# Projection and experts of a transformer tail put into one stage, with the projection's matmuls spread through the experts' chain

## The reference

```python
def _L1_ffn_ref(x, W, b, A, Bmat, LiMEs):        # x is the layer-normalised x
    H = jnp.einsum('btd,od->bto', x, W) + b       # d = o = 512
    z = jnp.einsum('btd,dr->btr', x, A)           # r = 32
    anchors = jnp.arange(1, T, 2)
    H_slice = H[:, anchors, :8]
    delta_slice = jnp.einsum('bar,er->bae', z[:, anchors], LiMEs)
    H_scale = jnp.maximum(jnp.max(jnp.abs(H_slice)), EPS)
    d_scale = jnp.maximum(jnp.max(jnp.abs(delta_slice)), EPS)
    logits = 0.5 * (H_slice / H_scale) + 0.5 * (delta_slice / d_scale)
    probs = softmax(logits)
    thresh = top_k(probs, 2)[0][..., -1:]
    weights = probs * sigmoid((probs - thresh) / 0.5)
    weights = weights / (sum(weights) + 1e-9)
    p_mix = jnp.einsum('bte,er->btr', repeat(weights, 2), LiMEs)
    return H + jnp.einsum('btr,ro->bto', z * p_mix, Bmat) * 0.5
```

## Time and profile before

| what | us |
|---|---|
| median of three runs (798.72 to 800.43) | 799.75 |
| the profiled execution | 799.84 |
| its span, from the first to the last instruction | 797.8 |
| TensorE busy in the span | 691.3 |
| VectorE | 622.4 |
| ScalarE | 482.2 |
| GpSimd | 364.8 |

### The profile page before, as it was taken

One profiled execution on the slowest core, in us unless ns is written; L12 is line 12 of the kernel. 1 busy time (PEld: TensorE's weight loads), 2 busy tenths in 40 slices (PEclk: granted clock), 3 DMA queues, 4 the chain that ended last, 5 costly groups with the idle time before them and its releaser, 6 DMA issues. The chain is left out here.

```text
span 797.8 us, 17690 instructions
## 1 busy us (share of the span) xinstructions
PE 691.3 (87%) x6633; PEld 358.0 (45%) x6633; DVE 622.4 (78%) x1031; ACT 482.2 (60%) x870; POOL 364.8 (46%) x271
## 2 busy tenths in 40 slices
PE   4999999999967875699999489999999999389944
PEld 2454455545545654244444144444444444145541
DVE  6888788888636676699998398999999999355456
ACT  3878876676436665476776167878788787422100
POOL 2000039999725563022112257767686767333100
PEclk9999999999999998799999779999999999779955
DMA  6235455656253320134332100000000000045305
GB/s 161 77 132 171 154 177 151 152 135 173 55 146 72 83 68 6 21 75 75 75 67 57 31 0 2 1 2 1 2 1 1 2 1 1 1 80 80 53 1 210
DMA packets 94183, 54.90 MB, mean 69 GB/s; under 512 B 78548, under 2 KB 78548, under 8 KB 94100
## 3 DMA queue, kind: packets, MB, share of 16 engines
q1 hardware_dynamic: 93348, 53.25, 26.7%
q10 hardware_dynamic: 752, 0.52, 0.3%
HBM read 32.20 MB, written 4.19 MB: 46 GB/s over the span
## 5 line engine op out<-in xcount | busy, mean ns | idle before, releaser
L1312 POOL TENSOR_TENSOR query_qn<-query_eq,query_rq 128x1024 f32<-128x1024 f32 x64 | 121.8, 1904 | 56.7 <-DVE query_rq L1246 54.9
L558 ACT ACTIVATE keys_ek<-keys_psK,keys_mk 128x512 f32<-128x512 f32 x128 | 86.9, 684 | 38.9 <-DVE keys_mk L411 37.0
L411 DVE TENSOR_REDUCE keys_mk<-keys_psK 128x2 f32<-128x1024 f32 x64 | 77.9, 1217 | 16.7 <-PE keys_psK L617 16.6
L1237 DVE TENSOR_REDUCE query_mq<-query_psQ 128x16 bf16<-128x1024 f32 x64 | 75.6, 1181 | 5.2 <-PE query_psQ L1380 5.0
L1243 DVE TENSOR_REDUCE query_lq<-query_eq 128x16 f32<-128x1024 f32 x64 | 77.2, 1207 | 2.6 <-ACT query_eq L1321 2.5
L1321 ACT ACTIVATE query_eq<-query_psQ 128x1024 f32<-128x1024 f32 x64 | 65.2, 1019 | 22.5 <-PE query_psQ L1393 22.5
L628 PE MATMUL keys_psT<-all_ident,keys_ek 128*128 128x128 f32 x512 | 70.8, 282 | 0.0
L1402 PE MATMUL query_psX<-all_ident,query_qn 128*128 128x128 f32 x512 | 70.7, 282 | 0.0
L1040 POOL TENSOR_SCALAR ff_hr<-ff_h,ff_qs 128x1376 f32<-128x1376 f32 x16 | 22.7, 1416 | 104.4 <-DVE ff_qs L1087 104.4
L640 PE MATMUL keys_psG<-keys_eT,keys_cT 128*64 128x512 f32 x256 | 69.0, 617 | 1.0 <-issue 0.9
L628 PEld LDWEIGHTS keys_psT<-all_ident,keys_ek 128*128 128x128 f32 x512 | 55.5, 142 | 28.2 <-issue 20.0
(11 more groups left out here) (246 smaller groups left out, 1438.6 us busy)
## 6 DMA issues: line engine op xcount, KB each, us to landing
all_ring<-in_L_ffn_w_down_dram SPq DMA_DIRECT2D x8, 688.0 KB, 4.7
all_ring<-in_L_ffn_w_gate_dram SPq DMA_DIRECT2D x10, 512.0 KB, 4.9
all_ring<-in_L_ffn_w_up_dram SPq DMA_DIRECT2D x10, 512.0 KB, 3.9
all_x_res<-in_x_dram SPq DMA_DIRECT2D x4, 1024.0 KB, 6.1
att_ctx_n<-in_ctx_dram SPq DMA_DIRECT2D x16, 256.0 KB, 2.9
out_dram<-all_x_res SPq DMA_DIRECT2D x16, 256.0 KB, 2.2
all_cf<-in_ctx_dram SPq DMA_DIRECT2D x15, 256.0 KB, 2.6
att_w_nat<-in_L_ffn_W_dram SPq DMA_DIRECT2D x4, 256.0 KB, 4.5
```

Of the source, the lines that this page charges most:

```text
L411: dve.tensor_reduce(mk[:, c, :], psK[c % 2][:, :, :], X, ALU.max, negate=True).then_inc(mk_ok, 1)
L558: act.activation(ek[t % 2][b][:, c, :], psK[c % 2][:, b, :], ACT.Exp, bias=mk[:, c, b:b + 1], accum_out=le[t % 2][:, b, c:c + 1]).then_inc ...
L1237: dve.tensor_reduce(mq[g % 2][:, :, 0:HEADS], psQ[g % 2][:, :, :].rearrange("p b (h d) -> p b h d", d=D), X, ALU.max, negate=True).then_in ...
L1312: pool.tensor_tensor(qn[m % 2][:, :, :], eq[m % 3][:, :, :], rq[m % 2][:, :].unsqueeze(2).broadcast_to([P, 2 * HEADS, D]), ALU.mult).then_ ...
```

## The change

One stage `projection_and_experts` takes the place of the two, and `x_T` is kept for all 16 tiles. Per tile TensorE does z (12 passes of 128 columns), then only the eight router columns of H in eight narrow passes, into `psR`. ScalarE copies both out (`zT`, `raw`). Of H itself ten tiles (`product_of`) are computed through two banks `psH`, four passes per tile of the loop and the rest between the steps of the chain; ScalarE copies them to `hb` and GpSimd adds them to the residual. H of the other six tiles goes straight into the bank in which `bm_parts` is added. `dl` is done for four tiles at a time in the loop. High parts are made four tiles ahead. GpSimd adds five products after its 16 bias additions and the other five only after `done_v` 5, the end of the chain. VectorE does `zp` of two groups at once, and the low part of the next group before the last results of a group. The core of the diff, with the new code of each engine:

```diff
-def projection(nc, a, k):
-def experts(nc, a, k):
+def projection_and_experts(nc, a, k):
+    FILL = 4
+    AHEAD = 3
+    product_of = [0, 1, 4, 8, 5, 9, 2, 6, 3, 7]
+    FIRST = 5
+    order = [4 * g + q for q in range(4) for g in range(4)]
+    added = [TILES + product_of.index(t) + 1 if t in product_of else t + 1 for t in range(TILES)]
+        x_T = s.sb("x_T", [P, TILES, 2 * NC, P], F16)
+        psD = [psA, psH[0], psH[1], psB]
+        w_head = k.WT[:, :, :, 0:EXPERTS]
...
+        def _(pool):
+            for t in range(TILES):
+                pool.wait_ge(xs_ok, t + 1)
+                pool.tensor_tensor(k.x[:, t, :], k.x[:, t, :], k.b_full[:, :], ALU.add).then_inc(b_ok, 1)
+            pool.wait_ge(b_ok, TILES)
+            for n in range(FIRST):
+                add_product(n)
+            pool.wait_ge(done_v, 5)
+            for n in range(FIRST, PRODUCTS):
+                add_product(n)
...
+        def _(act):
+            for i in range(AHEAD + 1):
+                high(i)
+            for i in range(TILES):
+                if i + AHEAD + 1 < TILES:
+                    high(i + AHEAD + 1)
+                act.wait_ge(z_ps, i + 1)
+                act.activation(zT[:, i, :], psR[:, 2 + i % 2, 0:P], ACT.Copy, scale=1.0 / W_SCALE).then_inc(z_ok, 1)
+                act.wait_ge(n_ps, i + 1)
+                act.activation(raw[:, i, :, :], psR[:, i % 2, 0:2 * EXPERTS].rearrange("p (m e) -> p m e", m=2),
+                               ACT.Copy).then_inc(raw_ok, 1)
+                if i % 3 == 2:
+                    product(i // 3)
+            product(5)
+            act.wait_ge(done_v, 3)
+            act.activation(e[:, :, :], lg[:, :, :], ACT.Exp).then_inc(act_ok, 1)
+            product(6)
+            act.wait_ge(done_v, 4)
+            act.activation(w[:, :, :], u[:, :, :], ACT.Exp, scale=-2.0).then_inc(act_ok, 1)
...
+        def _(dve):
+            for i in range(TILES):
+                low(i)
+                if i + 2 < TILES:
+                    normed(i + 2)
...
+            scaled(0)
+            scaled(1)
+            rest(0)
+            for q in range(4):
+                for g in range(3 if q < 2 else 2):
+                    result(4 * q + g)
                 if q < 3:
+                    rest(q + 1)
+                if q < 2:
+                    scaled(q + 2)
+                for g in range(3 if q < 2 else 2, 4):
+                    result(4 * q + g)
...
+                for c in range(NC):
+                    pe.matmul(head, hi[c], w_head[:, :, c, :], start=c == 0, stop=False, skip_group_check=True)
+                for c in range(NC):
+                    mm = pe.matmul(head[:, 0:EXPERTS], lo[c], w_head[:, 0, c, :], start=False, stop=c == NC - 1,
+                                   skip_group_check=True)
+                mm.then_inc(n_ps, 1)
+                if i < TILES - 1:
+                    products(FILL * i, FILL * i + FILL)
+                if i > 0 and i % 4 == 0:
+                    z_limes(i - 4, i)
...
             for n, t in enumerate(order):
+                bank = psD[n % 4]
+                if n in (1, 2):
+                    pe.wait_ge(hb_ok, PRODUCTS - 2 + n)
+                wait(pe, o_ok, n - 3)
+                if t not in product_of:
+                    for m in range(4 if n == 3 else 0, 3 * NC):
+                        projected(t, bank, m, False)
                 pe.wait_ge(z_fin, n // 4 + 1)
+                pe.matmul(bank[:, :], zs[:, t % 4, t // 4, :], k.bm_parts[:, :], start=t in product_of,
+                          stop=True).then_inc(d_ps, 1)
```

More of the change, by code:

```diff
@@ new lines, in _ @@
+                    normed(i + 2)
+            dve.memset(ones2[:, :], 1.0).then_inc(lnk, 1)
+            dve.memset(wf[:, :, :], 0.0).then_inc(lnk, 1)
+            n[0] += 2
+            dve.wait_ge(lnk, n[0])
+            dve.wait_ge(raw_ok, TILES)
+            link(dve.scalar_tensor_tensor(out=Hs[:, :, :], in0=raw[:, :, 0, :], scalar=1.0 / W_SCALE,
+                                          in1=k.b_full[:, 0:EXPERTS].unsqueeze(1).broadcast_to(TE), op0=ALU.mult, op1=ALU.add))
+            link(dve.scalar_tensor_tensor(out=Hs[:, :, :], in0=raw[:, :, 1, :], scalar=1.0 / W_SCALE, in1=Hs[:, :, :],
+                                          op0=ALU.mult, op1=ALU.add))
@@ new lines, in rest, with result @@
+            def rest(q):
+                dve.wait_ge(zs_ok, q + 1)
+                dve.tensor_tensor(zs[D:P, q, :, :], zp[D:P, q, :, :], zs[D:P, q, :, :], ALU.subtract).then_inc(z_fin, 1)
+            def result(m):
+                t = order[m]
+                dve.wait_ge(b_ok, added[t])
+                dve.wait_ge(d_ps, m + 1)
+                dve.scalar_tensor_tensor(out=k.x[:, t, :], in0=psD[m % 4][:, :], scalar=1.0 / W_SCALE,
+                                         in1=k.x[:, t, :], op0=ALU.mult, op1=ALU.add).then_inc(o_ok, 1)
@@ L1644, in _ @@
+            scaled(0)
+            scaled(1)
+            rest(0)
             for q in range(4):
+                for g in range(3 if q < 2 else 2):
+                    result(4 * q + g)
                 if q < 3:
-                    product(q + 1)
-                dve.wait_ge(zs_ok, q + 1)
-                dve.tensor_tensor(tiles(zs, q)[D:P], tiles(zp, q)[D:P], tiles(zs, q)[D:P], ALU.subtract).then_inc(z_fin, 1)
-                for n in range(4 * q, 4 * q + 4):
-                    dve.wait_ge(d_ps, n + 1)
-                    t = order[n]
-                    dve.scalar_tensor_tensor(out=k.x[:, t, :], in0=psD[n % 4][:, :], scalar=1.0 / W_SCALE,
-                                             in1=k.x[:, t, :], op0=ALU.mult, op1=ALU.add).then_inc(o_ok, 1)
@@ L1666, in _, with parts_of @@
-        @block.sync
-        def _(sp):
-            for n, t in enumerate(order):
-                sp.wait_ge(o_ok, n + 1)
-                sp.dma_start(out[t], k.x[:, t, :]).then_inc(store, 16)
-            sp.wait_ge(store, 16 * TILES)
+                    rest(q + 1)
[3 more added lines that the diff above has]
+                    result(4 * q + g)
         @block.tensor
         def _(pe):
-            for t in range(TILES):
-                mm = pe.matmul(psA[:, t * EXPERTS:(t + 1) * EXPERTS], k.zT[0:RANK, t, :], k.limesT[:, :],
-                               start=True, stop=True)
-            mm.then_inc(a_ps, 1)
+            def parts_of(t):
+                hi = [x_T[:, t, c, :] for c in range(NC)]
+                lo = [x_T[:, t, NC + c, :] for c in range(NC)]
+                return hi, lo
@@ new lines, in projected, with products @@
+            def projected(t, bank, m, stop):
+                hi, lo = parts_of(t)
+                xT, wt = ((hi, k.WT_hi), (hi, k.WT_lo), (lo, k.WT_hi))[m // NC]
+                return pe.matmul(bank[:, :], xT[m % NC], wt[:, m % NC, :], start=m == 0, stop=stop)
+            def products(first, last):
+                for j in range(first, last):
+                    n, m = j // (3 * NC), j % (3 * NC)
+                    if m == 0:
+                        wait(pe, hb_ok, n - 1)
+                    mm = projected(product_of[n], psH[n % 2], m, m == 3 * NC - 1)
+                    if m == 3 * NC - 1:
+                        mm.then_inc(h_ps, 1)
```

216 lines of the change are left out of this document (98 added, 118 removed).

## The result

The changed kernel takes 775.6 us in the median of four runs (774.49 to 777.45); beside it the kernel before took 799.24 (798.62 to 800.43). The ratio is 0.9702 with a 95% interval of 0.9685 to 0.9719: 3% faster. The forecast was 782.1 with a range of 777 to 789. The profiled execution took 775.0 us.

What follows compares the result with a forecast made beforehand. TensorE's queue was taken to carry nearly all the tail: from 701.13, 70.8 us of passes, 2.7 of low clock and 1.8 of waits reach 776.4; last result, store and surroundings make 782.1, likely cases 777 to 789.

Steps and rivals of the forecast that it cites:

- the fill covers the chain: VectorE chain, L1600 to L1626: 35 wide TensorE passes, 7.6 us, stand beside its 7.5 us, leaving some 0.3 us for hand-over.
- The rival of 814 us: From the chain's first link on: clock falls to 0.50, 148 wide passes cost 0.216 more each, 32.0 us; chance 0.04.
- router's heads: Eight narrow passes per tile in the loop: 128 at 0.056 us, 7.2 us, with bounds of 0.030 and 0.101 each.
- weights' spread: Spreading the experts' weights (L1691 before): 32 passes at 0.112 us, 3.6 us, with bounds of 0.050 and 0.160 each.
- dl, 32 passes: dl matmuls (L1676 before), 24 of them now in the projection: 0.112 us each, 3.6 us.
- low clock at the start: TensorE from the first z at 701.13 to 706.40: the lower clock costs half of 5.3 us, 2.7.
- waits: TensorE's remaining waits: 0.3 at the chain, 0.3 at wT copies, 0.2 around z_fin, 1.0 at the results; 1.8 us in all.
- the case at 787.9: Router's head passes each cost their weight load, 0.101 us, adding 5.8 us; chance 0.12.
- cheap small passes: Head passes at 0.030 us (3.3 less, 2.9 let through) and spread at 0.050 (2.0 less): 777.2; chance 0.15.
- these five additions: GpSimd's last five product additions, behind done_v 5, when VectorE mostly reads psum: costed at nothing.
- The feeding loop: VectorE and GpSimd preparing tiles: 2.21 us per tile against TensorE's 2.20, hence nothing on the sum.
- the slack at tile 15: Last tile of the loop: its transpose lands at 734.2, TensorE comes at 736.2, two microseconds of slack.

Runs made afterwards that it cites:

- e4: Changed kernel with the 44 wide passes between the chain's steps issued ahead of its first link: 789.22 us, ratio 0.9868 to the kernel before.
- e3: Changed kernel with each tile's eight narrow head passes done twice: 779.31 us, ratio 0.9745 to the kernel before.
- e2: Kernel before the change, with the spread's matmuls rotating over the row strips and the first product waiting for all four groups: 799.9 us (one run).
- e1: Changed kernel with the spread's matmuls in the old order, four in a row on the same row strip: 782.7 us (one run).
- e5: Changed kernel with GpSimd's last five additions no longer waiting for the chain's end: 778.28 us, ratio 0.9732 to the kernel before.
- e11: Changed kernel plus 18 unread warm-up passes, bias additions waiting for the third tile after their own, one product added before the chain: 777.9 us.
- e6: Changed kernel plus 18 unread wide TensorE passes while it would wait for the first transpose: 775.89 us, ratio 0.9702 to the kernel before.
- e10: The changed kernel again, unaltered, beside the runs with extra passes on the same chip: 777.70 us, ratio 0.9729 to the kernel before.
- e8: Changed kernel without the bias in the residual, GpSimd setting one element per tile instead of adding: 775.6 us (one run).

## Why the prediction was right or wrong

**Right: what bounds the kernel and where the gain comes from.** TensorE's idle time went, the clock stayed at 1.00, and the fill covers the chain: 35 passes stand in 737.20 to 744.71, 7.5 us, as worked out. e4 shows the worth of the passes between the links, 9.3 us of cover and some 3 of clock. The four wide passes of a tile, the z passes, the last result and the first hand-overs have their forecast sizes. The rival of 814 us counted 60 products after the first link; 50 stand there in the order, which makes 812, and e4 shows that it would not have come.

**The sum against the trace.** From TensorE's first z pass to its last the prediction has 701.13 to 776.56, 75.43 us; the trace has 699.67 to 769.95, 70.28. The difference of 5.15 by its terms:

| term | forecast | measured | difference |
|---|---|---|---|
| router's heads, 128 passes | 7.2 | 3.3 | -3.9 |
| weights' spread, 32 passes | 3.6 | 1.1 | -2.5 |
| dl, 32 passes | 3.6 | 4.0 | +0.4 |
| low clock at the start | 2.7 | 2.4 | -0.3 |
| waits (measured: what is left) | 1.8 | 2.9 | +1.1 |

The first two tiles took 5.88 us where two at the full clock take 3.47; that is the 2.4. Behind the last result the store took 2.43 us instead of 2.7, and the stage began 1.5 us sooner: together 773.2 instead of 780.0 for the span.

**The failed steps are the two prices of small passes.** The sum took 0.056 for a head pass, "the nearest row, which contains a full load of this kind; fewer columns cannot make it dearer unless the load itself does". It is 0.025 (e3), below even the lower bound of 0.030. The wrong step was to read 0.056 as what the weight load needs. The load is hidden behind its neighbours: one lasts 0.10 us in this trace too, and four head passes with their four loads begin 0.10 after each other (728.56, 728.66, 728.76 for the two groups and the fill). The columns fit as what costs 0.056 for a pass with 128 of them (0.056 x 2.4 GHz = 134 cycles); that was not tried by itself. Sixteen and eight columns cost 0.025 alike, the distance of the 64x64 passes in the earlier trace rows, a row that I had in hand and took as a bound, rounded up. The rule of the Trainium skill, "TensorE: Matmul & The Clock Gate", LDWEIGHTS, by which 128 columns of weights load in P/1.2 = 107 ns, describes one load's duration well (0.10 here) and not the rate of consecutive passes; the case at 787.9 was wrong by a factor of four in the price.

The spread was put at 0.112 with a lower bound of 0.050. It is 0.034 (1.10/32). I had seen that neighbouring passes use other row strips and gave it no number; e2 and e1 give it, a factor of 2.4 at either clock, strips and banks together. The rival "cheap small passes" (777.2, chance 0.15) is what came, and both of its prices were still too high.

**Waits: 1.8 against 2.9.** By the distances of starts the chain's links cost the 0.3 forecast, the copies of wT 0.27 (0.3 forecast) and a bank wait in the results 0.58 (1.0 forecast). The first `bm_parts` pass comes 0.67 late instead of 0.2, and two items are in no forecast: 0.66 before the second group's `bm_parts` pass, which waits for its `rest` too (752.78 to 753.65), and some 0.36 before the four groups of dl. The first `bm_parts` pass waits for `rest`, and `rest` took 1.26 instead of 0.69. That is the addition behind `done_v` 5 beside it: in e5, where none runs, that part is 0.57 shorter. The prediction put these five additions "behind done_v 5, when VectorE mostly reads psum", and cost them "at nothing"; `rest` reads sbuf. The same with the fifth addition before the chain: the first Hs step took 0.95 instead of 0.29, within the 0.55 to 1.3 us allowed. It cost nothing: in e11, where that step took 0.29, VectorE waited 0.71 us for dl instead.

**The feeding loop: right, and nearer than it looked.** A tile costs VectorE and GpSimd 2.01 us instead of the 2.21 that I had worked out: normed is stopped (1.37), low isn't (0.68), the addition takes 1.65 and the next begins 0.36 later. The Trainium skill, "SBUF — State Buffer", SBUF: two separate sides, has this stop for a VectorE instruction with one tensor input when it runs in a two-port mode; normed is stopped in the loop, and two `tensor_scalar` steps in e5, while no run shows the mode itself. TensorE's tile is 1.74 and a quarter of 1.0 for dl, 1.99 us. So both queues run at the same pace, and TensorE's 2.4 us of low clock gave the loop its slack. That is why the slack at tile 15 was the 2 us forecast (its low part ended at 726.26 and its z began at 731.36, with 3.1 for the transpose), and why e6, which takes the low clock away, wins 0.8.

**The range.** It was built from costs alone. The stage's start differs by up to 2.6 us between profiles of this one kernel (693.76, 694.43, 696.38), and a median by 2.1. The lower bound should have held that too. Which side of that bound a median falls on is partly chance: with the start of the kernel before, 1.5 us later, the profiled execution would have taken 776.5, still half a microsecond below the range, and e10's median of 777.7 lies inside it, with the same two prices wrong.

## What to carry to other kernels

Price a narrow matmul from the distance between starts of the narrowest passes in the trace, not from a weight load's duration or a wider pass, and let few-row f32 matmuls of one group rotate over the row strips and psum banks (the two were never tried apart). Before removing a loss on the bounding engine, compare the pace of the engine that feeds it: here the two were 1% apart, and 2.4 us of removed loss returned 0.8. A GpSimd addition of two sbuf tensors held up VectorE steps with two sbuf tensors, and `tensor_scalar` steps with one, until it ended; a reduce, a reciprocal and steps with a psum operand went on beside it. So put it beside those or beside waits, and count the steps that it would meet.

## What the runs showed of the hardware that I had not expected

- f16 passes of 128x128 weights with 16 or 8 moving columns follow each other at 0.025 us at the full clock, weight loads included.
- 32 f32 passes of eight rows and 128 columns: 1.17 us rotating over four strips (and four psum banks) and 2.81 on one strip (and bank) at a time at the full clock, 2.09 and 5.13 at the low one.
- TensorE busy for 2.8 us with eight-row passes alone was followed by 1.2 GHz from 754.77 to 758.18 while wide passes ran (e1); with 1.1 us of them, in the other runs that reached them at the full clock, it was not.
- TensorE came back from the wait of 12.5 us at 1.2 GHz and had its full clock again after 5.4 us of z, heads and fill (699.67 to 705.04); in e8 after 6.1.
- A VectorE `tensor_scalar` of 128x16, 0.17 us alone, took 0.80 beside a GpSimd addition (e5); a `tensor_reduce` of 128x128 took 0.29 beside one, as without.
